# A vision tower on one core: up tiles of the feed-forward projected during the gate's search, most of them kept in DRAM

## The chip, the core and the metric

The kernel runs on one core of a Trainium2 chip. A core has a matrix engine (PE, TensorE), a vector engine (DVE), a scalar engine (ACT), GpSimd (POOL), and a queue engine (SP) that here only issues DMAs. Operands lie in SBUF, results of PE in eight banks of PSUM. The metric is the device time of one execution in microseconds. Three runs of the kernel before took 1360.43 to 1363.68 us, 1361.9 us in the median.

## What is computed

The reference is a small vision tower over 64 images of 96 x 96 pixels: a patch tokenizer (36 tokens of 192 features an image), attention with 12 heads of 16 (phase B below), two attention layers with 12 heads of 64 (phases C and D), and a gated feed-forward. Only this last layer is touched. Cut to what matters (x is the normalized input, 64 x 36 tokens):

```python
pooled = x.mean(1)                                  # 64 x 192, one row an image
ck     = relu(pooled @ w1.T) @ w2.T                 # 64 x 3072 gate values
probs  = softmax(ck, -1)
mask   = zeros_like(probs).at[b, top_k(probs, 768)].set(1.0)
hidden = relu(x @ w_mfc.T) * mask[:, None, :]       # 64 x 36 x 3072
out    = x_residual + hidden @ w_proj.T
```

## The kernel before, in words

The kernel keeps the tokens of all images in SBUF as h (22 groups of 108 tokens, three images each). Phases B, C and D are the attention layers, each closed by `phase_end`, a barrier of all five engines. During phase D the normalized input of the feed-forward is written transposed, as a rounded high part `f_xh` and a low part `f_xl`, since PE multiplies in a rounded format and the kernel wants more digits.

Phase E is the selection. PE and ACT compute the gate values into banks 0 to 2, half of the 3072 values of an image on each of two partitions, DVE takes the maximum, ACT the exponent, DVE scales them (`f_p`, 128 x 1536, line 1744). Then the 768th largest is searched bit by bit, 30 steps in `vector_select` (lines 1747 to 1764): DVE counts the values that reach the candidate (line 1750, `f_eq`), PE adds the two halves' counts in one small matmul (line 1665, into bank 7), DVE decides the bit with three small operations and so forms the next candidate. After the steps come two counts, a scan for ties, and two operations that make the mask `f_scan`; PE transposes it in 12 blocks (line 1674) into banks 0 to 2, and ACT copies it into `f_maskT` (line 1701). Beside this, SP loads the up weights (3 MB with one half doubled; `load_weights`) and then, when POOL is through with them, the down weights (2.3 MB). ACT rounds both to the high part and POOL subtracts to get the low part (`f_wu`, `f_wd`). The barrier of phase E follows.

The feed-forward walks six units of 4, 4, 4, 4, 3 and 3 groups (432 columns of tokens, at the end 324 and 252), and in each 24 tiles t of 128 hidden features. A tile m has an up half (five matmuls, `up` in `tensor_mlp`, lines 1814 to 1818, banks m mod 4), then on DVE relu and mask in one operation (`f_hid`, line 1891), on ACT the high part (line 1921), on POOL the low part (line 1935), and on PE a down half (five matmuls, lines 1829 to 1834) that adds into banks 4 and 5. The order on PE is up of tile m, down of tile m - 3 (`LAG`). There are four buffers each of `f_hid`, its high and low part: DVE waits for the parts of tile m - 4, ACT and POOL for its down half. After a unit, ACT and DVE copy banks 4 and 5 to `f_oT` (`take`), PE transposes them back (`back`, line 1845, into banks 6 and 7), DVE adds to h (`finish`), and SP stores the groups (`store`). In what order an engine works is the order of the code; the waits are counts on semaphores.

```python
        for m in range(len(order) + self.LAG):
            if m < len(order):
                up(m)
            if m >= self.LAG:
                u, g0, n, t = order[m - self.LAG]
                down(m - self.LAG)
```

## Time and profile before

| | us |
|---|---|
| median of three runs | 1361.9 |
| the profiled execution | 1363.47 |
| its span, first to last instruction | 1361.2 |
| PE busy in the span | 1183.3 (87%) |
| DVE busy | 956.3 (70%) |
| ACT busy | 880.7 (65%) |
| POOL busy | 436.9 (32%) |
| moved by DMA | 30.27 MB |

A busy time is the sum over an engine's instructions; a share of the whole span mixes stages that differ. The page also cuts the span into 40 slices of 34 us, with busy tenths for each engine and the granted clock of PE in tenths of full speed. The chain of waits follows back from the last instruction to what released each step. The profiled execution took 1363.47 us, 2.3 us more than its span.

### The profile page before, as it was taken

The numbers are of one execution on the slowest core, as the hardware profiler recorded it, in microseconds if no ns is written. First come the engines' busy times: TensorE is split into PE (matmuls) and PEld (weight loads), VectorE is DVE, ScalarE is ACT, GpSimd is POOL, SyncE is SP. The second block draws the span as 40 slices with busy tenths as digits, with TensorE's granted clock in tenths as the row PEclk, the third lists the DMA queues.
The fourth block names the chain that finished last, engine by engine and source line by source line (L and its number), as shares of the span: only waits on it lengthen the run. The fifth ranks groups of instructions, "written<-read, shape, count | busy, mean of one in ns | idle before, by whom it ended". The sixth has DMA issues, their size and how long they took to land.

```text
span 1361.2 us, 25095 instructions
## 1 busy us (share of the span) xinstructions
PE 1183.3 (87%) x8302; PEld 1043.3 (77%) x8302; DVE 956.3 (70%) x2350; ACT 880.7 (65%) x3172; POOL 436.9 (32%) x467
## 2 busy tenths in 40 slices
PE   6988879868999999998699999999830089999998
PEld 4986657647888888897589989899710079999998
DVE  4669988865888898896478888888758833333333
ACT  1757788854999999987498998998731022222232
POOL 0000130204323333320343443443224035555555
PEclk8999999896999999999899999999965589999999
DMA  9202011000000000000000000000031000000000
GB/s 371 109 1 72 1 47 25 1 1 0 2 1 2 1 1 2 1 2 1 12 1 1 1 1 2 1 1 1 1 93 70 0 1 1 11 10 11 1 11 13
DMA packets 7849, 30.27 MB, mean 22 GB/s; under 512 B 2094, under 2 KB 4894, under 8 KB 6174
## 3 DMA queue, kind: packets, MB, share of 16 engines
q1 hardware_dynamic: 7724, 28.69, 6.2%
q8 instruction: 68, 1.11, 0.3%
q14 instruction: 57, 0.47, 0.1%
HBM read 26.92 MB, written 1.77 MB: 21 GB/s over the span
## 4 chain that ended last, share of the span: by engine, by line
PE 61%; DVE 9%; ACT 6%; issue 1%; POOL 1%; POOLq 0%; ACTq 0%; DVEq 0%
PE bank L1466 6%; PE bank L1431 6%; DVE f_eq L1750 4%; PE bank L1395 4%; PE bank L1457 4%; PE bank L1440 3%; PE bank L1415 3%; PE bank L1399 3%; PE bank L1396 3%; PE bank L1397 3%; PE bank L1398 3%; ACT t_p L1211 2%; PE bank L1814 2%; PE bank L1829 2%; PE bank L1816 2%; PE bank L1815 2%
## 5 line engine op out<-in xcount | busy, mean ns | idle before, releaser
L1211 ACT ACTIVATE t_p<-bank,t_nmax 108x108 f32<-108x108 f32 x792 | 267.2, 354 | 40.2 <-DVE t_nmax L740 39.4
L1935 POOL TENSOR_TENSOR f_hid_lo<-f_hid,f_hid_hi 128x432 fp32r<-128x432 f32 (+2 forms) x144 | 145.8, 1013 | 160.6 <-ACT f_hid_hi L1921 160.6
L1891 DVE SCALAR_TENSOR_TENSOR f_hid<-bank,f_maskT 128x432 f32<-128x432 f32 (+2 forms) x144 | 80.3, 558 | 165.6 <-PE bank L1818 164.4
L1047 POOL TENSOR_TENSOR t_sq<-t_raw 108x768 f32<-108x768 f32 x88 | 140.9, 1602 | 168.7 <-ACT t_raw L1151 167.7
L1921 ACT CAST f_hid_hi<-f_hid 128x432 fp32r<-128x432 f32 (+2 forms) x144 | 73.9, 513 | 181.1 <-DVE f_hid L1891 181.1
L1431 PE MATMUL bank<-t_kS,t_qT 128*108 128x216 f32 (+1 forms) x660 | 179.1, 386 | 3.3 <-DVE h L331 2.5
L1211 ACT ACTIVATION_READ_ACCUMULATOR t_p<-bank,t_nmax 108x1 f32 x792 | 166.1, 210 | 0.0
L758 DVE TENSOR_TENSOR t_p<-t_p,t_rinv 108x432 f32<-108x432 f32 x198 | 160.4, 810 | 6.8
L740 DVE TENSOR_REDUCE t_nmax<-bank 108x4 f32<-108x432 f32 x198 | 119.5, 603 | 59.2 <-PE bank L1431 58.8
L1440 PEld LDWEIGHTS bank<-ident,t_p 108*108 108x108 f32 x792 | 86.7, 132 | 54.7 <-ACT t_pT L1219 35.1
L1440 PE MATMUL bank<-ident,t_p 108*108 108x108 f32 x792 | 107.4, 258 | 22.2 <-ACT t_pT L1219 21.0
L1431 PEld LDWEIGHTS bank<-t_kS,t_qT 128*108 128x108 f32 x660 | 110.6, 175 | 8.9 <-DVE h L331 2.5
L1219 ACT COPY t_pT<-bank 108x432 f32<-108x432 f32 x198 | 104.1, 527 | 11.4 <-PE bank L1440 10.4
L736 DVE TENSOR_TENSOR t_raw<-t_raw,t_rn 108x768 f32<-108x768 f32 x88 | 85.0, 966 | 16.4 <-ACT t_rn L1178 10.2
L1151 ACT COPY t_raw<-bank 108x384 f32<-108x384 f32 x176 | 86.3, 493 | 15.0 <-PE bank L1399 14.9
L1457 PE MATMUL bank<-t_pT,t_v 108*64 108x108 f32 (+1 forms) x1584 | 84.9, 263 | 6.6 <-issue 6.5
L1055 POOL TENSOR_TENSOR t_xl<-t_xt,t_xh 128x108 fp32r<-128x108 f32 x44 | 18.6, 422 | 213.9 <-DVE t_xh L711 213.9
L1457 PEld LDWEIGHTS bank<-t_pT,t_v 108*64 108x64 f32 (+1 forms) x1584 | 61.8, 127 | 33.2 <-issue 29.6
L1415 PE MATMUL bank<-ident,t_raw 108*128 108x108 f32 x528 | 78.7, 258 | 7.8 <-ACT t_kS L1193 3.3
L1415 PEld LDWEIGHTS bank<-ident,t_raw 108*128 108x128 f32 x528 | 66.1, 143 | 15.8 <-ACT t_kS L1193 3.9
L1665 PE MATMUL bank<-f_count,f_both 128*128 128x1 f16 x30 | 5.6, 186 | 70.5 <-DVE f_eq L1750 70.5
L391 PE MATMUL bank<-A_w,A_x 128*108 128x193 f32 x352 | 64.6, 339 | 1.9 <-DVE A_w L311 1.9
(227 smaller groups left out, 3250.6 us busy)
## 6 DMA issues: line engine op xcount, KB each, us to landing
A_x<-in_x SPq DMA_DIRECT2D x5, 1728.0 KB, 18.6
A_w<-in_tok_w SPq DMA_DIRECT2D x5, 768.0 KB, 7.2
f_raw_down<-in_w_proj SPq DMA_DIRECT2D x1, 2304.0 KB, 8.4
out_tokens<-h SPq DMA_DIRECT2D x21, 81.0 KB
f_raw<-in_w_mfc SPq DMA_DIRECT2D x1, 1536.0 KB, 7.3
f_raw<-in_w_mfc SPq DMA_DIRECT2D x2, 768.0 KB, 12.2
W_raw<-in_wC SPq DMA_DIRECT2D x1, 1159.0 KB
W_raw<-in_wC SPq DMA_DIRECT2D x2, 579.5 KB
```

The costliest lines, as they stand in the source:

```text
L736: dve.tensor_tensor(v, v, r, ALU.mult).then_inc(s["qn"], 1)
L740: dve.tensor_reduce(b.nmax[:, 4 * c:4 * c + 4], self.sbank[(3 * g + c) % 2][0:GT, 0:4 * GT].rearrange("p (a n) -> p a n", n=GT), AX.X, ALU ...
L758: dve.tensor_tensor(p, p, b.rinv[:, sl].unsqueeze(2).to_broadcast([GT, 4, GT]), ALU.mult).then_inc(s["pn"], 1)
L1047: pool.tensor_tensor(sq, v, v, ALU.mult).then_inc(s["sq"], 1)
L1151: act.copy(b.raw[k][:, 384 * c:384 * c + 384], src[0:GT, 0:384]).then_inc(s["Qev"], 1)
L1211: act.activation(b.p[g % 2][:, m, :], self.sbank[(3 * g + c) % 2][0:GT, n * GT:(n + 1) * GT], ACT.Exp, bias=b.nmax[:, m:m + 1], accum_out= ...
L1219: act.copy(b.pT[:, 4 * c:4 * c + 4, :], src.rearrange("p (a n) -> p a n", a=4)).then_inc(s["Tev"], 1)
L1415: mm = pe.transpose(o, b.raw[k][:, 128 * (3 * u + n):128 * (3 * u + n + 1)], I[0:GT, 0:GT])
L1431: mm = pe.matmul(o[0:GT, n * GT:(n + per) * GT], b.qT[g % 2][:, hd // per, :], b.kS[g % 2][:, hd:hd + per, :], start=masked, stop=True, sk ...
L1440: mm = pe.transpose(t[0:GT, n * GT:(n + 1) * GT], b.p[g % 2][:, 4 * c + n, :], I[0:GT, 0:GT])
L1457: mm = pe.matmul(self.pv[n][lo:hi, t * GT:(t + 1) * GT], b.v[g % 4][:, self.vd * hd:self.vd * (hd + 1)], b.pT[:, hd, :], start=True, stop= ...
L1935: pool.tensor_tensor(self.hid_lo[m % 4][:, c], self.hid[m % 4][:, c], self.hid_hi[m % 4][:, c].bitcast(F32), ALU.subtract).then_inc(s["lo" ...
```

## The change

Of the tiles of units 0 to 3, those with t not a multiple of 3 (64 of 96) have their up half computed in the selection: two after the sum of the exponents, two behind each of the 30 totals, two behind the sums for the ties (`early`, banks 3 to 5 in turn). ACT applies relu and writes each to one of eight slots in SBUF; SP stores 56 of them to DRAM (`spill`), and the last eight, the first kept ones of unit 0, stay in the slots. In the feed-forward SP reads the 56 back into the slots as they come free (`bring_back`), and for such a tile DVE multiplies the slot by the mask, which it reads from banks 0 to 2 of PSUM, in the order of the tiles. Up halves of the other tiles (`live`) use banks 6 and 3 in turn, later 0, 1, 6 and 3. The first two live up halves are computed in the selection too.

The up weights come in thirds of 1024 columns; two thirds are loaded by `load`, at the start of phase D, the last by `load_weights` at the start of the selection, and the down weights right after it without the wait for POOL. ACT rounds two thirds before the exponents and one after; the down weights are rounded and subtracted in four parts, between the evictions. The barrier of phase E is gone. The turning back of a unit is split into two lots of two groups (t = 1 and 6), in bank 7 (the last one in bank 0). The wait of PE for two casts at the start of phase C is dropped, and several semaphores are joined; the tokenizer's `s_wide` becomes a second count of `s_rows`.

```diff
-    phases = ("B", "C", "D", "E")
+    phases = ("B", "C", "D")
...
+        third = HID // 3
+        raw_of = lambda p, n: [p(f"f_raw{n}{m}", [128, third]) for m in two]
+        over = Plan_at(late, late.at)
+        self.w2 = over("f_w2", [12, HID])
+        self.raw = [raw_of(small, 0), raw_of(over, 1)]
...
+        unit = self.UNIT * GT
+        slot = lambda p, n: p(f"f_slot{n}", [128, unit])
+        self.slots = [slot(small, n) for n in range(5)]
...
+        self.raw_down = plan("f_raw_down", [128, HT, DIM])
+        self.raw.append(raw_of(plan, 2))
...
+        self.slots.append(slot(plan, 5))
+        below = Plan_at(small, first_raw_at)
+        self.slots += [slot(below, n) for n in range(6, self.SLOTS)]
...
+        self.order = list(self.tiles())
+        self.spilled = [m for m, (u, g0, n, t) in enumerate(self.order) if u < self.EARLY_UNITS and t % 3]
+        first = [m for m in self.spilled if self.order[m][0] == 0]
+        self.early = [m for m in self.spilled if self.order[m][0]] + first[self.SLOTS:] + first[:self.SLOTS]
+        self.stores = len(self.early) - self.SLOTS
+        self.stayed = nc.dram_tensor("spilled", (self.stores, 128, unit), F32, kind="Internal").ap()
+        self.moved = [sem(f"F_moved{n}") for n in range(self.SLOTS)]
...
+        self.load_third(sp, ins, 0, "rawU")
+        self.load_third(sp, ins, 1, "rawU")
+    def load_third(self, sp, ins, n, name):
+        cols = slice(n * HID // 3, (n + 1) * HID // 3)
+        a, b = self.raw[n]
+        sp.dma_start(a[:, :], ins["w_mfc"][0:128, cols]).then_inc(self.loaded[name], 16)
+        sp.dma_start(b[0:LO, :], ins["w_mfc"][128:192, cols]).then_inc(self.loaded[name], 16)
+        sp.dma_start(b[LO:128, :], ins["w_mfc"][128:192, cols]).then_inc(self.loaded[name], 16)
...
-        sp.dma_start(self.raw[0][:, :], ins["w_mfc"][0:128, :]).then_inc(self.loaded["rawU"], 16)
-        sp.dma_start(self.raw[1][0:LO, :], ins["w_mfc"][128:192, :]).then_inc(self.loaded["rawU"], 16)
-        sp.dma_start(self.raw[1][LO:128, :], ins["w_mfc"][128:192, :]).then_inc(self.loaded["rawU"], 16)
-        sp.wait_ge(self.s["wlo"], 2)
+        self.load_third(sp, ins, 2, "lastU")
         sp.dma_start(self.raw_down[:, :, :], ins["w_proj"]).then_inc(self.loaded["wdn"], 16)
...
+    def spill(self, sp):
+        for j in range(self.stores):
+            u, g0, n, t = self.order[self.early[j]]
+            w = self.columns(g0, n)
+            sp.wait_ge(self.s["relu"], j + 1)
+            sp.dma_start(self.stayed[j, :, 0:w], self.slots[self.slot(j)][:, 0:w])\
+              .then_inc(self.moved[self.slot(j)], 16)
+        for n in range(self.SLOTS):
+            sp.wait_ge(self.moved[n], 16 * self.stored(n))
+    def bring_back(self, sp, unit):
+        for q in range(self.SLOTS, len(self.spilled)):
+            m = self.spilled[q]
+            u, g0, n, t = self.order[m]
+            if u == unit:
+                w, k = self.columns(g0, n), self.slot(self.stores + q)
+                sp.wait_ge(self.s["hid"], self.spilled[q - self.SLOTS] + 1)
+                sp.dma_start(self.slots[k][:, 0:w], self.stayed[self.early.index(m), :, 0:w])\
+                  .then_inc(self.moved[k], 16)
...
+        def early(j):
+            u, g0, n, t = self.order[self.early[j]]
+            pe.wait_ge(s["low"], 2 * (t // self.THIRD + 1))
+            if j >= 3:
+                pe.wait_ge(s["relu"], j - 2)
+            self.project_up(pe, self.bank[3 + (j + 2) % 3], g0, n, t).then_inc(s["early"], 1)
+        pe.wait_ge(s["pre"], 2)
+        across(1, sm[:, 14:15], start=True, stop=True).then_inc(s["across"], 1)
+        early(0)
+        early(1)
         pe.wait_ge(s["padding"], 2)
         for n in range(self.BITS):
             pe.wait_ge(s["count"], n + 1)
             pe.matmul(self.bank[7][:, 0:1], self.both[:, :], self.count[:, 0:1], start=True, stop=True)\
               .then_inc(s["total"], 1)
+            early(2 * n + 2)
+            early(2 * n + 3)
         pe.wait_ge(s["eq"], 2)
         across(1, sm[:, 17:18], start=True, stop=False)
-        across(2, sm[:, 18:19], start=False, stop=True).then_inc(s["need"], 1)
-        pe.wait_ge(s["mask"], 1)
+        across(2, sm[:, 18:19], start=False, stop=True).then_inc(s["across"], 1)
+        for j in range(2 * self.BITS + 2, len(self.early)):
+            early(j)
+        pe.wait_ge(s["relu"], len(self.early) - 2)
+        self.up(pe, 0)
+        self.up(pe, 1)
+        pe.wait_ge(s["eq"], 6)
...
+        def high(n):
+            act.wait_ge(*((self.loaded["rawU"], 96) if n < 2 else (self.loaded["lastU"], 48)))
+            cols = slice(n * HID // 3, (n + 1) * HID // 3)
+            for m in range(2):
+                act.copy(self.wu[2 * m][:, cols], self.raw[n][m][:, :]).then_inc(s["high"], 1)
+        act.wait_ge(s["layers"], 1)
         act.activation(self.c1[:, 0:IMAGES], self.bank[6][0:12, 0:IMAGES], ACT.Relu, scale=1.0 / TOKENS)\
            .then_inc(s["c1s"], 1)
-        act.wait_ge(s["nmax"], 1)
+        high(0)
+        high(1)
+        act.wait_ge(s["pre"], 1)
         for c in range(self.half // 512):
             act.activation(self.p[:, 512 * c:512 * c + 512], self.bank[c][:, :], ACT.Exp, bias=sm[:, 7:8],
                            accum_out=sm[:, 8 + c:9 + c]).then_inc(s["exp"], 1)
-        act.wait_ge(self.loaded["rawU"], 48)
-        act.copy(self.wu[0][:, :], self.raw[0][:, :]).then_inc(s["whi"], 1)
-        act.copy(self.wu[2][:, :], self.raw[1][:, :]).then_inc(s["whi"], 1)
-        act.wait_ge(s["ck"], self.half // 512)
-        act.wait_ge(self.loaded["wdn"], 16)
-        act.copy(self.wd[:, :, 0:DIM], self.raw_down[:, :, :]).then_inc(s["dhi"], 1)
+        high(2)
+        for j, m in enumerate(self.early):
+            u, g0, n, t = self.order[m]
+            w, k = self.columns(g0, n), self.slot(j)
+            act.wait_ge(s["early"], j + 1)
+            if j >= self.SLOTS:
+                act.wait_ge(self.moved[k], 16 * len(range(k, j, self.SLOTS)))
+            elif j >= 6:
+                act.wait_ge(s["low"], 2)
+            act.activation(self.slots[k][:, 0:w], self.bank[3 + (j + 2) % 3][:, 0:w], ACT.Relu).then_inc(s["relu"], 1)
+            if j in (8, 12, 16, 20):
+                act.wait_ge(s["layers"], 1 + self.half // 512)
+                act.wait_ge(s["low"], 4)
+                act.wait_ge(self.loaded["wdn"], 16)
+                part = self.part(j // 4 - 2)
+                act.copy(self.wd[:, part, 0:DIM], self.raw_down[:, part, :]).then_inc(s["high"], 1)
...
+        for n in range(3):
+            cols = slice(n * HID // 3, (n + 1) * HID // 3)
+            for m in range(2):
+                pool.wait_ge(s["high"], 2 * n + m + 1)
+                pool.tensor_tensor(self.wu[2 * m + 1][:, cols], self.raw[n][m][:, :],
+                                   self.wu[2 * m][:, cols].bitcast(F32), ALU.subtract).then_inc(s["low"], 1)
...
+    def live(self, i):
+        turns = [m for m in range(len(self.order)) if m not in self.spilled]
+        of = []
+        for n, m in enumerate(turns):
+            masks = n < self.EARLY_UNITS * HT - len(self.spilled) + 6
+            of.append((6, 3)[n % 2] if masks else (0, 1, 6, 3)[n % 4])
+        past = [turns[n] for n in range(i) if of[n] == of[i]]
+        if not past and of[i] < 3:
+            past = [self.spilled[-1]]
+        return turns[i], self.bank[of[i]], past[-1] if past else None
+    def up(self, pe, i):
+        m, bank, past = self.live(i)
+        u, g0, n, t = self.order[m]
+        if past is not None:
+            pe.wait_ge(self.s["hid"], past + 1)
+        self.project_up(pe, bank, g0, n, t).then_inc(self.s["up"], 1)
...
+        turns = [m for m in range(len(order)) if m not in self.spilled]
         for m in range(len(order) + self.LAG):
-            if m < len(order):
-                up(m)
+            if m in turns[2:]:
+                self.up(pe, turns.index(m))
             if m >= self.LAG:
                 u, g0, n, t = order[m - self.LAG]
                 down(m - self.LAG)
-                if t == 1 and u:
-                    back(u - 1, self.UNITS[u - 1])
-        back(len(self.UNITS) - 1, self.UNITS[-1])
+                if u and t in (1, 6):
+                    back(u - 1, self.halves_of(u - 1)[t > 1])
+        for js in self.halves_of(len(self.UNITS) - 1):
+            back(len(self.UNITS) - 1, js)
...
+            if m in self.spilled:
+                k = self.spilled.index(m)
+                self.arrived(dve, k)
+                dve.wait_ge(s["mTev"], 2 * q + 2)
+                dve.tensor_tensor(split(self.hid[m % 4]), split(self.slots[self.slot(self.stores + k)]),
+                                  spread(self.bank[q][:, at:at + ni]), ALU.mult).then_inc(s["hid"], 1)
+            else:
+                i, bank, past = self.live(lives)
+                lives += 1
+                dve.wait_ge(s["up"], lives)
+                dve.wait_ge(s["mTev"], 2 * q + a + 1)
+                dve.scalar_tensor_tensor(out=split(self.hid[m % 4]), in0=split(bank), scalar=0.0,
+                                         in1=spread(self.maskT[:, t, i0:i0 + ni]), op0=ALU.max, op1=ALU.mult)\
+                   .then_inc(s["hid"], 1)
...
+        self.bring_back(sp, 0)
+        self.bring_back(sp, 1)
+        for u, n in enumerate(self.UNITS):
+            self.bring_back(sp, u + 2)
+            g0 = sum(self.UNITS[:u])
+            for g in range(g0, g0 + n):
+                rows = min(GT, total - g * GT)
+                sp.wait_ge(self.s["h"], 2 * (g + 1))
+                sp.dma_start(flat[g * GT:g * GT + rows, :], self.h[0:rows, g, :]).then_inc(stored, 16)
...
```

## Rows read from the trace of the kernel before

**Rows 1.** The page, 40 slices of the span: PE busy tenths, granted clock.

```profile
PE   6988879868999999998699999999830089999998
...
PEclk8999999896999999999899999999965589999999
```

**Rows 2.** Busy us by stretch: length, PE, PEld, DVE, ACT, POOL, PEclk, DMA share, GB/s.

```profile
160.00:170.00 10.00, 7.32 (x68) 5.69 (x69) 9.15 (x17) 7.38 (x36) 0.00 (x0) 1.00 0.01 2
1040.00:1060.00 20.00, 1.50 (x8) 0.84 (x8) 17.70 (x41) 0.00 (x0) 9.61 (x2) 0.50 0.00 0
1151.10:1199.04 47.94, 47.94 (x250) 45.82 (x249) 17.06 (x33) 13.70 (x25) 26.83 (x25) 1.00 0.03 8
1158.00:1159.00 1.00, 1.00 (x7) 0.96 (x6) 0.96 (x4) 0.00 (x0) 0.34 (x1) 1.00 0.56 161
```

**Rows 3.** Timeline (start us, us, engine, line, operation, out<-in), a search step.

```profile
1078.04 0.19 PE L1665 MATMUL bank<-f_count,f_both 128*128 128x1 f16 x1 [2.31 <-DVE f_eq L1750]
...
1078.66 1.81 DVE L1750 TENSOR_SCALAR_CACHE_REDUCE f_eq<-f_p,f_word 128x1536 bf16<-128x1536 f32 x1
...
1081.16 1.81 DVE L1750 TENSOR_SCALAR_CACHE_REDUCE f_eq<-f_p,f_word 128x1536 bf16<-128x1536 f32 x1
```

**Rows 4.** Timeline, one tile of unit 0 in the feed-forward.

```profile
1124.48 0.36 PE L1814 MATMUL bank<-f_xh,f_wu 128*128 128x432 f32 x1
...
1124.97 1.11 POOL L1935 TENSOR_TENSOR f_hid_lo<-f_hid,f_hid_hi 128x432 fp32r<-128x432 f32 x1 [0.85 <-ACT f_hid_hi L1921]
...
1125.66 0.61 DVE L1891 SCALAR_TENSOR_TENSOR f_hid<-bank,f_maskT 128x432 f32<-128x432 f32 x1 [1.36 <-PE bank L1818]
...
1126.44 0.36 PE L1814 MATMUL bank<-f_xh,f_wu 128*128 128x432 f32 x1
```

**Rows 5.** The chain of waits (start us, us, what), turning back a unit.

```profile
1154.06 0.87 PE bank L1845 x8
```

**Rows 6.** Timeline, the first matmuls of the feed-forward.

```profile
1097.40 0.65 ACT L1701 COPY f_maskT<-bank 128x256 f32<-128x256 f32 x2 [0.21 <-PE bank L1674]
...
1098.67 0.56 PE L1815 MATMUL bank<-f_xh,f_wu 128*128 128x432 f32 x1
...
1101.91 0.37 PE L1814 MATMUL bank<-f_xh,f_wu 128*128 128x432 f32 x1
...
1103.89 0.36 PE L1829 MATMUL bank<-f_hid_hi,f_wd 128*128 128x432 f32 x1
```

**Rows 7.** Groups by line and shape, feed-forward: busy us, mean ns | idle before.

```profile
L1935 POOL TENSOR_TENSOR f_hid_lo<-f_hid,f_hid_hi 128x432 fp32r<-128x432 f32 x96 | 107.2, 1118 | 132.7 <-ACT f_hid_hi L1921 132.7
...
L1891 DVE SCALAR_TENSOR_TENSOR f_hid<-bank,f_maskT 128x432 f32<-128x432 f32 x96 | 58.3, 607 | 126.0 <-PE bank L1818 126.0
...
L1921 ACT CAST f_hid_hi<-f_hid 128x432 fp32r<-128x432 f32 x96 | 53.1, 553 | 135.9 <-DVE f_hid L1891 135.9
```

**Rows 8.** Timeline, PE near the end of phase D.

```profile
971.43 3.45 PE L1466 MATMUL bank<-oD,t_oT 128*108 128x192 f32 x12 [1.28 <-ACT t_oT L1226]
```

**Rows 9.** The page's DMA issues: out<-in, count, KB each, us to landing.

```profile
f_raw_down<-in_w_proj SPq DMA_DIRECT2D x1, 2304.0 KB, 8.4
```

**Rows 10.** Timeline, a stretch of phase B, then the first part of the selection.

```profile
151.91 5.10 POOL L489 TENSOR_TENSOR wC_lo<-W_raw,wC_hi 128x2318 fp32r<-128x2318 f32 x1 [48.25 <-ACT wC_hi L468]
...
154.46 3.01 DVE L758 TENSOR_TENSOR t_p<-t_p,t_rinv 108x432 f32<-108x432 f32 x1
...
1004.19 0.69 ACT L1685 ACTIVATE f_p<-bank,f_small 128x512 f32<-128x512 f32 x1 [7.37 <-DVE f_small L1738]
...
1007.37 1.02 DVE L1744 TENSOR_SCALAR f_p<-f_p,f_small 128x1536 f32<-128x1536 f32 x1
...
1010.51 2.75 ACT L1689 CAST f_wu<-f_raw 128x3072 fp32r<-128x3072 f32 x1 [4.20 <-DMA f_raw<-in_w_mfc]
...
1013.40 6.69 POOL L1706 TENSOR_TENSOR f_wu<-f_raw,f_wu 128x3072 fp32r<-128x3072 f32 x1 [17.60 <-ACT f_wu L1689]
...
1013.66 1.81 DVE L1750 TENSOR_SCALAR_CACHE_REDUCE f_eq<-f_p,f_word 128x1536 bf16<-128x1536 f32 x1
```

182 lines of the change are left out of this document (91 added, 91 removed).

## The prediction

> **What bounds the kernel now.** I read the slices of the page first [rows 1]. The slices in which PE falls to 3, 0 and 0 tenths are the selection; behind them come some 260 us of feed-forward with PE at 8 or 9. The busy times by stretch say the same [rows 2]: from 1040 to 1060 us DVE is busy for 17.7 of 20 us and PE for 1.5, at a granted clock of 0.50 (the lower level, 1.2 GHz); from 1151.10 to 1199.04 us, unit 1 of the feed-forward, PE is busy throughout at 1.00 (2.4 GHz), while POOL has 26.8 of 47.9 us. So there are two bounds side by side: a serial search on DVE, in which PE has nothing to do, and then PE alone. The timeline of one search step [rows 3]: a count of 1.81 us on DVE, 0.19 us PE, two small DVE operations, and the next count starts 2.50 us after the last. Thirty steps are 75 us of nearly free PE.
>
> A tile of the feed-forward [rows 4]: the first up matmuls of neighbouring tiles start at 1124.48 and 1126.44, 1.96 us apart, for ten matmuls at a pitch of 0.196 us. A group of five (one up or one down half) is 0.98 us. Check: unit 1 took 47.94 us [rows 2]; less 0.87 us of turning back [rows 5] it is 47.07 / 24 = 1.961 us for a tile. At the lower clock the pitch is 0.36 us: nine of them lie between 1098.67 and 1101.91 us [rows 6]; a group is 1.80 us.
>
> **The change, part by part.**
>
> (a) Up halves moved. 64 of the 96 up halves of units 0 to 3 go into the search. They are all 432 columns wide: 64 x 0.981 = 62.8 us less on PE behind the search. PE is the bound there, so it counts in full if no other engine becomes the bound. Three tiles (one live, two kept) now take PE 4 groups, 3.92 us. POOL needs 3 x 1.118 = 3.35 us, DVE 3 x 0.607, ACT 3 x 0.553 [rows 7]. POOL has 0.57 us left in 3.92. By the order of the code POOL may be up to four tiles ahead of the down half, and a live tile's chain (0.61 + 0.55 + 1.12 us and hops, some 2.5 us) must be over before PE has done its next four groups (3.9 us). It fits.
>
> (b) What they cost in the search. PE gets two tiles behind each total: 10 x 0.196 + 0.19 = 2.15 us in a step of 2.50 us, at the upper clock. That leaves 0.35 us. At the lower clock it would be 10 x 0.36 + 0.19 = 3.8 us: each step 1.3 us and more longer. Which level is granted decides the case. Less than 4 us of continuous work brought a matmul from 0.56 to 0.37 us at 1101.91 us [rows 6]. The clock stood at 1.00 in a stretch where PE was busy for 7.32 of 10 us [rows 2]; the search would be 86% busy with gaps of 0.35 us. After a gap of 1.28 us twelve matmuls took 3.45 us, the lower level [rows 8]. From about 1007 us PE works without a pause (tiles 0 and 1 at the lower clock, 3.6 us, end near 1010.7; the first total is due after the scaling at 1007.37, 1.02 us, and a count of 1.81, near 1010.4 [rows 10]), so I put 0.3 us on the start, with 1.5 us as the upper bound. The total matmul itself may be quicker at the upper clock: bounds 0 and half of its 0.19 us in each of 30 steps; I take 0.05 x 30 = 1.5 us gained. If tiles crowd the total by 0.25 us in each step, 7.5 us are lost: that is the other bound.
>
> (c) ACT and the stores. ACT gets two evictions a step, each like the 0.55 us conversion of 432 columns [rows 7], and in four steps a quarter of the down weights' copy (4608 columns; by the 2.75 us for 3072 [rows 10] some 1.0 us): at most 2.1 us of 2.50. The stores are 221 KB each; two a step are 177 GB/s. A burst of stores of the output ran at 161 GB/s at a DMA share of 0.56, so up to 287 GB/s when busy throughout [rows 2]. They fit, and eight slots give 10 us of slack. The returns are asked for eight kept tiles ahead (some 15 us), against 8.4 us for the landing of ten times the bytes [rows 9]. On SP the returns for unit u+2 stand ahead of the stores of unit u, which delays only output that nobody waits for: from unit 2 on there are none. Both transfers: nothing on the path.
>
> (d) Weights. Up weights in thirds: two of the loads (2 MB) move into phase D, on queues that are idle there; the six conversions on ACT (about 1 us each, a third of 2.75 [rows 10]) start near 996.9 us: four end by 1000.9, before ACT's first exponent at 1004.19. POOL's six subtractions (a third of 6.69 us, 2.25 us each) run from about 998 to 1012 us. Here is the only collision that I see. The row at 154.46 us [rows 10] shows a DVE multiply with both inputs in SBUF take 3.01 us in place of 0.61, up to 157.0, just as the POOL operation that began at 151.91 ended. The scaling of p at 1007.37 us (1.02 us for 1536 elements, twice the pace of the counts) is on the chain, and POOL's fourth subtraction ends near 1007.0, its fifth starts near 1007.3. Bounds: 0, or two whole POOL operations, 4.5 us. I take one, +2.3 us. The counts themselves took 1.81 us while POOL was in its 6.69 us operation as well as without it [rows 3, 10], so they cost nothing.
>
> The Trainium skill has the rule, in "SBUF — State Buffer", section "Who interferes with whom": a DVE instruction in a 2-port mode, or with two SBUF inputs, and a GpSimd one that reads SBUF exclude each other, whoever is first. The row agrees for two inputs. Applied to kept tiles: their multiply reads a slot in SBUF and the mask in PSUM, so by that rule POOL is left alone; with the mask in SBUF the sum would be 20 us worse (rival 2).
>
> (e) The start of the feed-forward. Before, four up halves were done at 1103.89 us and 284 groups were left. After, PE has two live up halves done and starts the downs when ACT, done with the masks at 1098.05 us [rows 6], has converted tile 0 (1098.6 us). At the lower clock, each down waiting for POOL: down 0 ends about 1100.5, down 1 at 1102.3, down 2 at 1103.3. Left: 288 - 64 - 2 - 3 = 219 groups. Gain against before, parts (a) and (e) together: (284 - 219) x 0.981 + (1103.89 - 1103.3) = 64.4 us. The tail of the selection on DVE stays as it is: four groups (tiles 62, 63, two live ones) run under it from 1088.4; even with the first at the lower clock they end before 1094.5. The mask transposes could then run at 1.4 in place of 2.8 us: 0 to -1.4, I take 0. The removed barrier is inside this part.
>
> (f) The rest: joined semaphores and the split turning back (same 8 transposes a unit, in two lots) cost nothing: each lot is followed by matmuls already released. In units 4 and 5 nothing changes but two banks for the first six tiles; there an up half waits for a multiply released three groups earlier.
>
> **Sum.** 1363.47 - 64.4 - 1.5 + 0.3 + 2.3 = 1300.2 us for the profiled execution. That one is 1.6 us above the median of its runs, 1361.9; on that scale the forecast is 1298.6, said as 1299. The unknown parts alone give 1293 to 1309 (lock -2.3/+2.2, crowded steps +9, transposes -1.4, faster totals -1.5, and some 1 us for the start).
>
> **Rivals.**
> 1. Steps crowded: PE's 2.15 us plus restart gaps exceed what is free before the next total. For: only 0.35 us of slack, and each tile waits for an eviction and a weight third. Against: the pitch of 0.196 held over whole units. +7.5 us and more, 1307 to 1312.
> 2. POOL becomes the bound of units 0 to 3. If kept tiles' multiplies (0.61) and POOL's operation exclude each other, three tiles take 3.35 + 1.2 = 4.6 us in place of 3.92: 32 x 0.65 = 21 us, 1320. Against: the live multiply (one input in PSUM) overlapped POOL at 1.12 us unstretched [rows 4, 7]. Store traffic at only 120 GB/s would cost about the same (12.4 MB in 103 us).
> 3. The change does not do what it says in time: the search stays at 1.2 GHz because PE stops at each total. A step is then about 3.9 us, 30 x 1.4 = 42 us given back: 1341.
> 4. Slower than before: the lower clock holds in the search and also in units 0 to 3, since PE waits there for POOL's results behind a short chain. A group costs 0.82 us more. After the 42 us of rival 3, 21 us are left, which 26 of the 219 groups use up: from there on the kernel is slower. With all 128 groups of units 0 to 3 it is +105 us, 1446. Against: 1.00 in every stretch of the feed-forward, and PE has work queued there.
>
> **How the numbers follow.** Forecast 0.74 (1293 to 1306), rival 1 0.10, rival 2 0.06, rival 3 0.06, rival 4 0.03, and 0.01 for a gain that vanishes by several of these. The range 1291 to 1313 takes the forecast with its bounds and rival 1. Faster by over 0.2% (what a measurement of this kernel can tell from no change) 0.96, within 0.01, slower 0.03.
>
> **What would show it.** Search steps still 2.45 to 2.50 us apart at a granted clock of 1.00; PE near 86% busy in them; the multiply of p stretched to about 3.3 us; units 1 to 3 at 24 + 8 groups, 31.4 + 0.9 = 32.3 us each, with PE full; POOL near 83% in them and still 1.12 us an operation; units 4 and 5 as before. Wrong it would be by steps of 2.7 us or more, a clock of 0.5 in the search, units over 34 us, or PE waiting for a returned slot.

## The result, and the profile after

The changed kernel took 1300.86 us in the median (1299.40 to 1303.14), the kernel before 1361.97: a ratio of 0.9553, 95% interval 0.9535 to 0.9570. The forecast was 1299, the range 1291 to 1313. The profiled execution took 1300.88 us, against 1300.2 of the sum.

The page after: span, the slices of PE and DVE, the granted clock and the share of the DMA engines, to be read beside [rows 1].

```profile
span 1299.1 us, 25559 instructions
...
PE   6998779895899999999869999999996898999998
...
DVE  5668989875788888889547888888874888444434
...
PEclk9999999897899999999989999999998899999999
DMA  9302002000000000000030000000003342334100
```

The two empty slices of PE are gone. DVE is as busy in the search as before, and the span ends 62 us sooner. The DMA engines, idle in the search before [rows 2], are at 2 to 4 tenths there and up to the end of unit 2 of the feed-forward.

Busy time by stretch (columns as in [rows 2]): the first two search steps, the other 28 steps, the tail of the selection, units 1 and 2 of the feed-forward.

```profile
1010.33:1016.74 6.41, 4.67 (x16) 3.86 (x16) 4.42 (x10) 1.48 (x3) 2.00 (x1) 0.54 0.26 97
1016.74:1086.40 69.66, 64.45 (x310) 52.36 (x309) 61.82 (x140) 33.61 (x61) 11.26 (x8) 1.00 0.46 169
1086.40:1097.28 10.88, 7.91 (x33) 6.82 (x32) 10.68 (x8) 2.12 (x4) 0.00 (x0) 0.84 0.01 2
...
1136.00:1168.14 32.14, 32.14 (x171) 30.75 (x169) 15.84 (x33) 13.42 (x25) 26.21 (x25) 1.00 0.38 112
1168.14:1200.30 32.16, 32.16 (x170) 30.77 (x169) 15.86 (x33) 13.46 (x25) 26.23 (x25) 1.00 0.42 121
```

The 28 steps take 69.66 us, 2.488 each, with PE at 93% and the upper clock; they carry 56 of the early tiles. Unit 1 takes 32.14 us in place of 47.94, PE full, POOL at 26.2 us, 82%. The forecast had 2.45 to 2.50 and 32.3. (From its turning back to the next, unit 3 took 33.73 us, 1200.30 to 1234.03: PE runs three tiles ahead, and in this stretch it does five up halves of unit 4, all live, where a unit of kept tiles has two.)

The groups of the feed-forward by line and shape, for [rows 7]: POOL's subtraction, DVE's multiply of a kept tile, DVE's relu and mask of a live one.

```profile
L2090 POOL TENSOR_TENSOR f_hid_lo<-f_hid,f_hid_hi 128x432 fp32r<-128x432 f32 x96 | 104.7, 1119 | 80.8 <-ACT f_hid_hi L2076 80.6
...
L2040 DVE TENSOR_TENSOR f_hid<-f_slot,bank 128x432 f32<-128x432 f32 x64 | 35.8, 595 | 1.3 <-ACT f_hid_hi L2076 0.8 <-POOL f_hid_lo L2090 0.5
L2047 DVE SCALAR_TENSOR_TENSOR f_hid<-bank,f_maskT 128x432 f32<-128x432 f32 x32 | 19.4, 608 | 59.3 <-PE bank L1922 52.5 <-POOL f_hid_lo L2090 5.6 <-ACT f_maskT L1806 1.3
```

POOL's operation is as long as before (1119 ns, 1118 before), kept multiplies beside it or not: with the mask in PSUM they do not meet.

The page's DMA issues, the stores and the returns, with the median us to landing.

```profile
spilled<-f_slot SPq DMA_DIRECT2D x56, 216.0 KB, 1.9
f_slot<-spilled SPq DMA_DIRECT2D x56, 216.0 KB, 2.5
```

The start of the search, on the timeline (start us, us, engine, line, operation; idle before it and who ended it in brackets), for [rows 3, 10].

```profile
1006.93 5.40 POOL L1814 TENSOR_TENSOR f_wu<-f_raw,f_wu 128x1024 fp32r<-128x1024 f32 x2 [0.15 <-ACT f_wu L1770]
1006.99 3.13 DVE L1850 TENSOR_SCALAR f_p<-f_p,f_small 128x1536 f32<-128x1536 f32 x1
...
1010.33 1.81 DVE L1856 TENSOR_SCALAR_CACHE_REDUCE f_eq<-f_p,f_word 128x1536 bf16<-128x1536 f32 x1
...
1012.30 0.16 PE L1743 MATMUL bank<-f_count,f_both 128*128 128x1 f16 x1 [1.74 <-DVE f_eq L1856]
...
1012.90 1.81 DVE L1856 TENSOR_SCALAR_CACHE_REDUCE f_eq<-f_p,f_word 128x1536 bf16<-128x1536 f32 x1
...
1015.71 0.56 PE L1922 MATMUL bank<-f_xh,f_wu 128*128 128x432 f32 x1
```

POOL began 0.06 us before DVE, and the scaling of p took 3.13 us in place of 1.02: the collision of part (d). PE had by then finished tiles 0 and 1 at the lower clock (0.56 us a matmul) and stood idle for 1.74 us until the delayed first total at 1012.30. The next two tiles ran at the lower clock again (the last of their matmuls at 1015.71), with the second total behind them, for which DVE waited 1.57 us: the second count begins at 1012.90 and the third at 1016.74, 3.84 us later.

Stage by stage, all from the timelines (us; the first row before, the second after, the last the difference):

| | first matmul of the selection to the scaling | scaling to first count | 30 steps | tail to the mask transposes | from there to the last addition | sum |
|---|---|---|---|---|---|---|
| before | 11.45 | 1.23 | 75.06 | 10.89 | 264.87 | 363.50 |
| after | 11.45 | 3.34 | 76.07 | 10.88 | 199.93 | 301.67 |
| difference | 0 | +2.11 | +1.01 | 0 | -64.94 | -61.83 |

The sum of a row, from the first matmul of the selection to the last addition to h, is called the stretch below. It leaves out what lies before the selection, which the edits hardly touch: the selection began between 993.7 and 997.9 us in the executions profiled, in no order that follows the edits. Still it is one execution of each kernel, and the granted clock differs from one to the next: what that does to single steps is told under e1_no_lock.

### The profile page after: what moved, and what is told of

Same layout as the page of the kernel before. It is cut to its first block, busy times and chain, and to the rows that moved or that the text cites. A ratio compares the mean times of both kernels' runs of the same rounds, so it can differ in the third digit from the quotient of the medians.

```text
span 1299.1 us, 25559 instructions
## 1 busy us (share of the span) xinstructions
PE 1191.0 (92%) x8302; PEld 1042.0 (80%) x8302; DVE 953.1 (73%) x2350; ACT 913.1 (70%) x3243; POOL 437.0 (34%) x477
## 3 DMA queue, kind: packets, MB, share of 16 engines
q1 hardware_dynamic: 24460, 53.47, 12.4%
## 4 chain that ended last, share of the span: by engine, by line
PE 59%; DVE 9%; ACT 7%; issue 2%; POOL 1%; POOLq 0%; DVEq 0%; ACTq 0%
PE bank L1463 7%; PE bank L1428 6%; PE bank L1392 4%; DVE f_eq L1856 4%; PE bank L1454 4%; PE bank L1437 3%; PE bank L1412 3%; PE bank L1396 3%; PE bank L1393 3%; PE bank L1395 3%; PE bank L1394 3%; ACT t_p L1208 2%; PE bank L1965 2%; PE bank L1961 2%; PE bank L1966 2%; PE bank L1962 2%
## 5 line engine op out<-in xcount | busy, mean ns | idle before, releaser
L2047 DVE SCALAR_TENSOR_TENSOR f_hid<-bank,f_maskT 128x432 f32<-128x432 f32 (+2 forms) x80 | 41.4, 518 | 100.3 <-PE bank L1922 92.9
L1792 ACT ACTIVATE f_slot<-bank 128x432 f32<-128x432 f32 x64 | 34.0, 531 | 49.0 <-PE bank L1922 49.0
```

## The experiments

All are edits on the changed kernel. The table has the median time, the ratio to the kernel before with its interval, and the stretch of the profiled execution with its difference to that of the changed kernel (301.67 us).

| run | us | ratio | stretch, us |
|---|---|---|---|
| changed kernel | 1300.86 | 0.9553 (0.9535 to 0.9570) | 301.67 |
| e3_all_live | 1361.67 | 0.9984 (0.9973 to 0.9994) | 362.90, +61.23 |
| e4_three_units | 1316.75 | 0.9660 (0.9646 to 0.9674) | 316.61, +14.94 |
| e1_no_lock | 1297.39 | 0.9513 (0.9501 to 0.9525) | 297.76, -3.91 |
| e2_mask_sbuf | 1302.86 | 0.9555 (0.9543 to 0.9567) | 302.76, +1.09 |
| e5_three_a_step | 1312.63 | 0.9627 (0.9614 to 0.9640) | 312.58, +10.91 |
| e10_one_a_step | 1332.93 | 0.9770 (0.9757 to 0.9783) | 333.11, +31.44 |
| e6_no_dram | 1302.24 | 0.9551 (0.9538 to 0.9564) | 301.29, -0.38 |
| e8_late_thirds | 1305.59 | 0.9571 (0.9556 to 0.9586) | 308.55, +6.88 |
| e11_barrier_back | 1301.85 | 0.9540 (0.9527 to 0.9553) | 302.16, +0.49 |
| e9_gap_filled | 1301.41 | 0.9546 (0.9533 to 0.9559) | 301.95, +0.28 |
| e7_more_kept | 1295.00 | 0.9496 (0.9483 to 0.9509) | 293.97, -7.70 |

**Is the gain the moved PE work, and all of it?** Two kernels keep the rest of the change and take early tiles away.

e3_all_live: no tile is kept.

```diff
-    EARLY_UNITS = 4
+    EARLY_UNITS = 0
...
+        act.wait_ge(s["low"], 4)
+        act.wait_ge(self.loaded["wdn"], 16)
+        for n in range(4):
+            act.copy(self.wd[:, self.part(n), 0:DIM], self.raw_down[:, self.part(n), :]).then_inc(s["high"], 1)
```

(The four down conversions stand alone, since there are no evictions to put them between.)

> Everything of the change but the early tiles: thirds of the weights, no barrier, two live up halves in the selection, split turning back; no tile is kept. The theory that the gain is PE work moved: 64 x 0.981 = 62.8 us come back, less 1.3 us of the stretched step and plus 1 to 2 us of a cold start of the feed-forward: 1363 to 1364, so the rest of the change is worth nothing or costs 1 to 2 us (2.1 of it the locked scaling). Rival (the barrier, the four-part weights and the start carry part of the gain): clearly under 1360.

e4_three_units:

```diff
-    EARLY_UNITS = 4
+    EARLY_UNITS = 3
...
-        pe.wait_ge(s["relu"], len(self.early) - 2)
+        pe.wait_ge(s["relu"], len(self.early) - 1)
```

> The changed kernel with early tiles for units 0 to 2 alone: 48 in place of 64, 40 stored. Theory (each early half is worth its 0.981 us of PE behind the search, wherever it stands): 16 x 0.981 = +15.7 us, 1316.6; steps stay 2.49 us, the last eight are empty. Rival (the gain saturates because POOL or the returns limit the units): clearly less than +15.7.

Without kept tiles the kernel is back within 0.2% of the kernel before, a little under the 1363 to 1364 us expected. Neither run has the stretched second step, so the tiles are counted by the last column but one of the stage table, from the mask transposes to the last addition (199.93 us in the changed kernel). It is 262.18 us in e3_all_live, 62.25 us more for 64 tiles, 0.973 each; the sum had 62.8. In e4_three_units it is 216.12 us, 16.2 more for 16 tiles, 1.01 each. By both, and by e10_one_a_step below, the gain is proportional to the groups that are moved, within the 1 us or so that the clock at the start of the feed-forward can shift, and nothing saturates. What is left of the -64.94 us, 2.69, came with the rest of the change (two live up halves in the selection, no barrier); its parts were not told apart. All the rest together, with the +2.1 us of the collision in it, is -0.60 us, 362.90 against 363.50.

**Does the collision cost what it seems to?** e1_no_lock lets POOL wait for the scaled p before its last two up subtractions.

```diff
         for n in range(3):
...
+            if n == 2:
+                pool.wait_ge(s["pre"], 4)
```

> One line more than the changed kernel: POOL holds back its two subtractions of the last third of the up weights until DVE has scaled p. In the changed kernel the scaling took 3.13 us in place of 1.02 while POOL worked from 1006.93 on, and the second search step began 3.84 us after its first, at the lower clock. Port theory: the scaling is back at 1.02 us (-2.1 us), PE then has no idle 1.7 us before the first total, so the next step is not stretched either (-1.3 us); together -3.4 us, about 1297.4 us. Rival A (the stretch of step 1 has nothing to do with the delay, PE is simply at the lower clock there): -2.1 us, 1298.8. Rival B (something else than POOL slows the scaling): 0, 1300.9.

The timeline of its first steps:

```profile
1007.78 1.02 DVE L1852 TENSOR_SCALAR f_p<-f_p,f_small 128x1536 f32<-128x1536 f32 x1
...
1008.88 4.70 POOL L1816 TENSOR_TENSOR f_wu<-f_raw,f_wu 128x1024 fp32r<-128x1024 f32 x2 [1.32 <-DVE f_p L1852]
...
1009.00 1.81 DVE L1858 TENSOR_SCALAR_CACHE_REDUCE f_eq<-f_p,f_word 128x1536 bf16<-128x1536 f32 x1
...
1011.82 1.81 DVE L1858 TENSOR_SCALAR_CACHE_REDUCE f_eq<-f_p,f_word 128x1536 bf16<-128x1536 f32 x1
...
1014.95 1.81 DVE L1858 TENSOR_SCALAR_CACHE_REDUCE f_eq<-f_p,f_word 128x1536 bf16<-128x1536 f32 x1
```

The scaling is at 1.02 us with POOL starting behind it, and the kernel is faster by 0.4%. That settles what slowed the scaling, 2.1 us. But the second half of the expectation failed: the first two steps are 2.82 and 3.13 us long, since PE still works at the lower clock there, so of the 1.3 us only 0.5 came back, and without any delay the cold start still costs 1.0 us. Nor is the delay what makes it dear. e4_three_units has the same code up to this point, the same scaling of 3.13 us and the same idle 1.74 us of PE before the first total. Its second and third count:

```profile
1012.18 1.81 DVE L1858 TENSOR_SCALAR_CACHE_REDUCE f_eq<-f_p,f_word 128x1536 bf16<-128x1536 f32 x1
...
1014.67 1.81 DVE L1858 TENSOR_SCALAR_CACHE_REDUCE f_eq<-f_p,f_word 128x1536 bf16<-128x1536 f32 x1
```

Its second step is 2.49 us long: the matmuls behind the first total already ran at the upper clock (granted 0.91 from 1009.62 to 1014.67). In the other executions with two tiles a step and the delayed scaling, the second step was 3.39 (e6_no_dram) to 3.85 us. So the stretch of this step is a matter of when the clock rises, and that differs from one execution to the next.

The rest of the 3.9 us came from the start of the feed-forward (1.4 us), where this execution had no fall of the clock. This cannot be put down to the edit: e2_mask_sbuf and e5_three_a_step, without it, had no fall there either. Three microseconds of that start, by stretch (columns as in [rows 2]), first in e1_no_lock:

```profile
1101.00:1104.00 3.00, 3.00 (x16) 2.72 (x15) 0.72 (x2) 0.56 (x1) 3.00 (x4) 1.00 0.60 147
```

Then in the changed kernel, at 0.68:

```profile
1103.00:1106.00 3.00, 3.00 (x12) 2.83 (x11) 0.11 (x1) 0.60 (x2) 3.00 (x4) 0.68 0.59 147
```

**Is the mask read from PSUM what keeps POOL free?** e2_mask_sbuf reads it from SBUF.

```diff
-                                  spread(self.bank[q][:, at:at + ni]), ALU.mult)
+                                  spread(self.maskT[:, t, i0:i0 + ni]), ALU.mult)
```

> The changed kernel, with the mask of the kept tiles read from its copy in SBUF in place of PSUM; same numbers computed. Port theory: this multiply now has two inputs in SBUF and excludes POOL's operation, so three tiles take POOL and DVE 3 x 1.119 + 2 x 0.595 = 4.55 us in place of 3.92 us of PE: 32 x 0.63 = 20 us more, 1321 us, and unit 1 some 37 us in place of 32.1. Rival (the source of the mask does not matter, as DVE has 50% idle): 0, 1301.

The two groups in its feed-forward, up to the end of unit 3:

```profile
L2090 POOL TENSOR_TENSOR f_hid_lo<-f_hid,f_hid_hi 128x432 fp32r<-128x432 f32 x95 | 124.8, 1350 | 61.8 <-ACT f_hid_hi L2076 61.8
...
L2040 DVE TENSOR_TENSOR f_hid<-f_slot,f_maskT 128x432 f32<-128x432 f32 x64 | 70.0, 1131 | 0.8 <-ACT f_hid_hi L2076 0.8
```

They do meet: POOL's mean goes from 1119 to 1350 ns and DVE's from 595 to 1131. But this costs the kernel 1.1 us of the stretch and nothing that the timed ratio tells, not 20 us. (The 1.1 us are too few: this execution had no fall of the clock at the start of the feed-forward. From the third live up half to the last addition it took 193.90 us, the changed kernel 191.79: 2.1 us are the price, and the timed ratio cannot tell so little.) I had counted POOL's operation and DVE's two as one after the other, 4.55 us for three tiles. From one turning back to the next (1137.26, 1169.95, 1202.65) a unit takes 32.70 us in place of 32.16, 4.09 us for three tiles in place of 4.02 (turning back included), and three of POOL's operations are 4.05 us: they lose 0.23 us each, while the loss of DVE, which has time to spare, is larger. So POOL, busy for 31.6 of the 32.7 us, is just at the bound, and the 20 us of the prediction were far off. With the mask in PSUM each of the two has its own length, as the rows of the changed kernel above show.

**How much does a step hold?** e5_three_a_step puts three tiles behind each of the first 20 totals.

```diff
-            early(2 * n + 2)
-            early(2 * n + 3)
+            for j in range(3 * n + 2, min(3 * n + 5, 62)):
+                early(j)
```

> The changed kernel with the same 64 early tiles, but three behind each of the first 20 totals and none behind the last ten. Theory (a step is as long as the longer of DVE's 2.49 us and PE's groups plus its total): 3 x 0.981 + 0.18 = 3.12 us in the first 20, so +0.63 x 20 = +12.7 us, about 1313.5; this is what crowded steps cost. Rival (PE's work hides further, for it may run behind the next count): 0, 1301.

One of its steps:

```profile
1031.06 0.18 PE L1745 MATMUL bank<-f_count,f_both 128*128 128x1 f16 x1
...
1031.29 0.17 DVE L1865 SCALAR_TENSOR_TENSOR bank<-bank,f_bits 128x1 uint32<-128x1 f32 x1 [0.79 <-PE bank L1745]
...
1031.68 1.81 DVE L1858 TENSOR_SCALAR_CACHE_REDUCE f_eq<-f_p,f_word 128x1536 bf16<-128x1536 f32 x1
...
1034.74 1.81 DVE L1858 TENSOR_SCALAR_CACHE_REDUCE f_eq<-f_p,f_word 128x1536 bf16<-128x1536 f32 x1
```

The total starts at 1031.06, right behind the third tile's matmuls, and DVE waits 0.79 us for it: a step of 3.06 us (1031.68 to 1034.74), just three groups of 0.98 and 0.12 us. Two groups and the total leave some 0.4 us of a step of 2.49. The 30 steps take 88.16 us in place of 76.07, 12.1 us more, near the 12.7 expected (the stretch shows 10.9, as the start of the feed-forward had no fall of the clock here); the empty last ten steps give nothing back. This is rival 1 at work: it begins somewhere between two and three tiles a step.

e10_one_a_step asks for the other side.

```diff
-    EARLY_UNITS = 4
+    EARLY_UNITS = 2
...
-            early(2 * n + 2)
-            early(2 * n + 3)
+            early(n + 2)
...
-        pe.wait_ge(s["relu"], len(self.early) - 2)
+        pe.wait_ge(s["relu"], len(self.early))
```

> Early tiles for units 0 and 1 alone (32), one behind each total, so that PE has 0.98 + 0.18 us in a step of 2.49 us. It asks what clock is granted with half the work. If the clock is held by long enough pauses alone (1.3 us here), the steps are at the lower level: a tile then takes 1.80 us and still fits, the steps stay 2.50 us, and the time is 1300.9 + 32 x 0.981 = 1332.3 us less the 1.3 us of the stretched step. If the upper clock holds, the same time: only the granted clock tells the two apart. A third outcome, that totals wait for a slow tile, would give more than 1334.

Two stretches of its search:

```profile
1020.00:1040.00 20.00, 15.45 (x48) 10.93 (x48) 17.75 (x41) 5.20 (x9) 2.78 (x2) 0.66 0.24 89
...
1060.00:1080.00 20.00, 13.39 (x49) 9.37 (x48) 17.76 (x41) 5.82 (x10) 2.79 (x2) 0.82 0.13 45
```

The granted clock is 0.66 and 0.82 in the mean, so both levels occur within the search, while steps stay at 2.49 us. The time is that of 32 tiles less: from the mask transposes to the last addition it is 232.50 us, 32.6 more, 1.02 each. (Of this some part is the clock, which was lower here at the start of the feed-forward; the 31.44 us of the stretch are less because no step is stretched.) One tile a step is not hurt by the lower clock (five matmuls of 0.36 us fit), but two are only free at the upper one, which PE, at 93%, kept for all 28 steps of the changed kernel. Rival 3 needed a fall of the clock there, and the short stop at each total did not bring it.

**Are the transfers free?** e6_no_dram issues neither stores nor returns. ACT and DVE no longer wait for slots to be stored or filled. The kept tiles of the feed-forward then multiply whatever a slot holds, so their part of the result is left out of the computation.

```diff
-            sp.wait_ge(self.s["relu"], j + 1)
-            sp.dma_start(self.stayed[j, :, 0:w], self.slots[self.slot(j)][:, 0:w])\
-              .then_inc(self.moved[self.slot(j)], 16)
...
-                sp.wait_ge(self.s["hid"], self.spilled[q - self.SLOTS] + 1)
-                sp.dma_start(self.slots[k][:, 0:w], self.stayed[self.early.index(m), :, 0:w])\
-                  .then_inc(self.moved[k], 16)
...
-            eng.wait_ge(self.moved[k], 16 * (self.stored(k) + q // self.SLOTS))
+            eng.wait_ge(self.s["relu"], len(self.early))
```

> The changed kernel without the 56 stores and the 56 returns: the slots are overwritten and the feed-forward multiplies what stands in them, so this part of the computation is wrong in its values and the same in its instructions. Theory (24.8 MB of transfers lie wholly beside the work): within 0.5 us of 1300.9. Rival (they cost something by late returns, or by slowing the engines' SBUF accesses): 2 us or more faster.

From 1136 to 1230 us (units 1 to 3), first e6_no_dram, then the changed kernel:

```profile
1136.00:1230.00 94.00, 94.00 (x495) 90.14 (x494) 45.02 (x95) 37.79 (x71) 76.32 (x71) 1.00 0.04 12
```

```profile
1136.00:1230.00 94.00, 94.00 (x497) 90.07 (x495) 44.66 (x94) 38.08 (x71) 76.39 (x71) 1.00 0.35 101
```

The DMA share is the column that moves; the busy times of the engines are the same within 1%, and so is the ratio. The 0.38 us of the stretch lie in the second search step (3.39 us in place of 3.84), which varies with the clock; from the mask transposes on it took 199.99 us against 199.93.

**Does the sooner load matter?** e8_late_thirds loads all three thirds at the start of the selection.

```diff
-        self.load_third(sp, ins, 0, "rawU")
-        self.load_third(sp, ins, 1, "rawU")
...
+        self.load_third(sp, ins, 0, "rawU")
+        self.load_third(sp, ins, 1, "rawU")
         self.load_third(sp, ins, 2, "lastU")
```

> The changed kernel with all three thirds of the up weights loaded at the start of the selection, none in phase D. Theory (the sooner loads are on the path: ACT converts two thirds before the exponents, in the order of its code): they land some 7 us after the selection begins, the conversions (3.9 us) end near 1007 in place of 1000.2, the exponents start 3 to 4 us later than 1003.81, and the collision of the scaling with POOL stays: 1304 to 1305. Rival (the loads were early for nothing, as other work covers them): 1301.

```profile
1006.08 3.88 ACT L1770 CAST f_wu<-f_raw 128x1024 fp32r<-128x1024 f32 x4 [11.42 <-DMA f_raw<-in_w_mfc]
...
1009.87 0.68 ACT L1779 ACTIVATE f_p<-bank,f_small 128x512 f32<-128x512 f32 x1
...
1013.05 2.04 DVE L1850 TENSOR_SCALAR f_p<-f_p,f_small 128x1536 f32<-128x1536 f32 x1
```

Yes. ACT gets its first third at 1006.08, 12.4 us after the first matmul of the selection (993.65), and the exponents wait behind its four conversions, until 1009.87; the scaling of p comes at 1013.05, 19.4 us after that matmul in place of 11.45. The stretch is 6.9 us longer, more than expected, because I had put the landing at 7 us. The median is 1305.6, 4.7 us more; the ratios say 2.5 us, with intervals that overlap. Against e11_barrier_back, timed beside the same runs of the kernel before, the intervals do not overlap (0.9556 to 0.9586, and 0.9527 to 0.9553), though that kernel has an extra barrier. So the thirds at the start of phase D are the better ones; the size lies between 2.5 and 7 us.

**The barrier.** e11_barrier_back has `phase_end` of all five engines again.

```diff
-    phases = ("B", "C", "D")
+    phases = ("B", "C", "D", "E")
...
         F.tensor_select(pe)
+        phase_end(pe, "E")
         F.tensor_mlp(pe)
```

> The changed kernel with the barrier of all five engines behind the selection put back, SP's part behind its last store. Theory (the barrier is short, and only the first multiply, which now starts after the first of six mask copies, is held back until the last): the first down half comes 1.0 to 1.5 us later, 1302.2. Rival (nothing, since ACT's copies hold everything back anyway): 1300.9. Rival (SP's last store, at the end of a chain of DMAs, is waited for by all): 1303 or more.

```profile
1099.34 1.53 PE L1765 MATMUL bank<-ident,f_scan 128*128 128x128 f32 x12 [0.95 <-DVE f_scan L1892]
...
1103.25 0.58 PE L1966 MATMUL bank<-f_hid_hi,f_wd 128*128 128x432 f32 x1 [2.38 <-ACT f_hid_hi L2081]
```

The first down half comes 3.91 us after the first transpose, in the changed kernel 2.94 (1097.28 to 1100.22): the barrier does hold it back by 1.0 us. To the last addition 0.5 us are left of it, and the timed ratios overlap. What the barrier costs, 0 to 1 us, this measurement cannot tell from nothing.

**What lowers the clock in the tail?** Here the trace of the changed kernel did not fit my picture. Its PE in the tail of the selection and at the start of the feed-forward:

```profile
1090.13 0.61 PE L1725 MATMUL bank<-f_small,f_halves 128*128 128x1 f32 x4 [2.02 <-DVE f_eq L1876]
...
1090.88 0.36 PE L1919 MATMUL bank<-f_xh,f_wu 128*128 128x432 f32 x1
...
1091.07 0.37 PE L1920 MATMUL bank<-f_xl,f_wu 128*128 128x432 f32 x1
...
1091.95 0.56 PE L1918 MATMUL bank<-f_xh,f_wu 128*128 128x432 f32 x1
...
1092.31 0.56 PE L1919 MATMUL bank<-f_xh,f_wu 128*128 128x432 f32 x1
...
1094.79 0.36 PE L1921 MATMUL bank<-f_xh,f_wu 128*128 128x432 f32 x1
...
1097.28 1.53 PE L1760 MATMUL bank<-ident,f_scan 128*128 128x128 f32 x12 [0.95 <-DVE f_scan L1887]
...
1100.22 0.46 PE L1961 MATMUL bank<-f_hid_hi,f_wd 128*128 128x432 f32 x1 [1.41 <-ACT f_hid_hi L2076]
```

After an idle time of 2.02 us (from 1088.11 to 1090.13) the next matmuls are still at the upper clock, 0.19 us apart at 1090.88 and 1091.07. Then, in the midst of continuous work, the pitch goes to 0.36 us (1091.95, 1092.31), and back near 1094.8. In e1_no_lock the same gap was followed by the lower clock at once:

```profile
1088.33 0.81 PE L1725 MATMUL bank<-f_small,f_halves 128*128 128x1 f32 x4 [2.04 <-DVE f_eq L1878]
...
1089.50 0.56 PE L1921 MATMUL bank<-f_xh,f_wu 128*128 128x432 f32 x1
```

e9_gap_filled moves two tiles into the idle time.

```diff
+        early(2 * self.BITS + 2)
+        early(2 * self.BITS + 3)
         pe.wait_ge(s["eq"], 2)
...
-        for j in range(2 * self.BITS + 2, len(self.early)):
+        for j in range(2 * self.BITS + 4, len(self.early)):
```

> The changed kernel, with tiles 62 and 63 put ahead of the sums for the ties in place of behind them, so that PE has no idle 2.0 us there. In the changed kernel PE ran at the lower clock from about 1091.3 to 1094.6 us, in the midst of matmuls, after that gap, and again from 1101.5 to 1104.8 at the start of the feed-forward. Clock theory: no fall in the tail (granted 1.00), which costs or gains nothing as DVE is the bound there; if the second fall also hangs on it, the feed-forward is 1.3 us shorter: 1299.6. Rival (the falls have other causes): the tail at 0.84 mean as before, 1300.9.

Its first 6.4 us of the tail, the time behind them, and a stretch of the start of the feed-forward:

```profile
1086.29:1092.70 6.41, 6.33 (x33) 5.41 (x31) 6.34 (x5) 2.13 (x4) 0.00 (x0) 1.00 0.01 3
1092.70:1097.18 4.48, 0.03 (x2) 0.01 (x1) 4.35 (x4) 0.00 (x0) 0.00 (x0) 1.00 0.00 0
1098.00:1104.00 6.00, 4.82 (x16) 3.90 (x15) 3.36 (x6) 4.17 (x11) 3.42 (x4) 0.50 0.34 92
```

The fall in the tail is gone, in this one execution. But the gap is only moved: PE is now idle for nearly all of the 4.48 us behind it, and in the six microseconds at the start of the feed-forward the clock is at the lower level, where it costs. Nothing is gained, and what makes the clock fall where it does stays open.

**A better version.** e7_more_kept puts the three things together: POOL waits for the scaling, tiles 62 and 63 go into the gap, and four more tiles are kept, computed where PE was idle behind the sums.

```diff
-        self.spilled = [m for m, (u, g0, n, t) in enumerate(self.order) if u < self.EARLY_UNITS and t % 3]
+        self.spilled = [m for m, (u, g0, n, t) in enumerate(self.order) if u < self.EARLY_UNITS and (t % 3 or (u and t == 12) or (u == 3 and t == 18))]
...
-        pe.wait_ge(s["relu"], len(self.early) - 2)
         self.up(pe, 0)
+        pe.wait_ge(s["relu"], len(self.early))
```

> Three edits on the changed kernel: POOL's last two up subtractions wait for the scaling of p; tiles 62 and 63 go ahead of the sums for the ties, into the 2.0 us in which PE waits; and four more tiles are kept (68), computed in the tail of the selection, where PE still has idle time under DVE's scan. Theory: -3.5 us of the first (as measured), -4 x 0.981 = -3.9 us of PE work, and the clock does not fall in the tail: about 1293.5, 1292.5 if the start of the feed-forward is at the upper clock. Rival (six groups behind the sums end after the mask is ready and delay it, or five kept tiles in a row make PE wait for POOL): 1297 or more.

The tail of its selection, and unit 2:

```profile
1084.98:1095.90 10.92, 10.34 (x53) 9.21 (x52) 10.72 (x9) 4.26 (x8) 0.00 (x0) 1.00 0.09 34
1164.50:1195.72 31.22, 31.22 (x165) 29.87 (x164) 15.77 (x33) 13.48 (x25) 26.21 (x25) 1.00 0.45 132
```

PE is busy for 10.34 of the 10.92 us of the tail, at the upper clock throughout, and a unit with 17 kept tiles is one group shorter (31.22 us). 1295.0 us is 0.6% less than the changed kernel, with intervals that do not touch; the stretch is 7.7 us shorter, the timed median 5.9. Most of this is POOL's wait. Against e1_no_lock, which has that alone, the stretch is 3.8 us shorter, as 4 x 0.98 would have it, but the timed intervals of the two overlap (0.9501 to 0.9525, and 0.9483 to 0.9509).

## Why the prediction was right

- **(a) and (e), moved halves and start: -64.4 foreseen, -64.94 measured.** e3_all_live and e4_three_units confirm the price of a half. Counted from the first mask transpose (the selection ended 2.7 us later than in the kernel before), I had down 0 ending after 5.95 us and down 2 after 8.75. Down 0 ended after 4.9, since the transposes ran at the upper clock (1.53 us in place of 2.82), which I had put at 0, and down 2 after 8.14, with the clock at the lower level from about 1101.5 to 1104.8. The 0.6 us that the start was better than the sum are about the whole difference between -64.4 and -64.94.
- **(b) the search: -1.2 foreseen, +1.0 measured.** Both terms were mis-sized. The total is only 0.012 us a step sooner at the upper clock, 0.35 us in all and not 1.5. And the cold start cost 1.3 us and not 0.3: I had counted tiles 0 and 1 at the lower clock, but tiles 2 and 3 ran at it too, with the second total behind them. The delay of (d) is not the reason, since without it the cost was 1.0 us (e1_no_lock), and with it none in e4_three_units. The bound of 1.5 held it.
- **(c) stores and returns: 0 foreseen, 0 measured** (e6_no_dram). They landed in 1.9 and 2.5 us. Of PE's share in the steps, 93% and not 86%, a part is only how a row counts: the last matmul before a pause has 0.35 us and not its pitch of 0.20. Ten pitches and 0.12 us for the total are 2.08 of 2.49 us, 84%.
- **(d) weights: +2.3 foreseen, +2.11 measured,** by the mechanism named; e1_no_lock shows that it is POOL. POOL's operation had begun only 0.06 us before the scaling, so an equally good account of the change could have had none of this loss; I took one operation, near the middle of the bounds, and that it came out is in part luck. In e8_late_thirds, where the scaling began in the midst of a row of POOL's operations, it took 2.04 us, so 1.0 us was lost and not a whole operation. The row that I took for a model [rows 10] I also misread: the multiply of 154.46 us ended at 157.47, 0.46 us behind POOL's operation and not with it.
- The rule of the Trainium skill cited there ("SBUF — State Buffer", section "Who interferes with whom") has POOL and DVE exclude each other. The scaling fits it: its 2.11 us of delay is about the length of one POOL operation (2.25 us). For a multiply with two inputs in SBUF e2_mask_sbuf does not: POOL's operations lost 0.23 us each, where full exclusion would have set three tiles at 4.55 us and 4.09 was measured. What is measured is a slowing of both, and my 20 us for rival 2 rested on the exclusion.
- **(f)** Unit 4 took 35.78 us from turning back to turning back, 35.67 before (1296.46 to 1332.13): 0.1 us, so nothing to speak of, as said.
- **Rivals 3 and 4** needed a lower clock under two tiles a step. It stayed at 1.00 from the third step on, but in e10_one_a_step, with half of that work, it did not.

That the sum came so near, 1300.2 for the profiled execution against 1300.88, is in part luck. Within the stretch the forecast was 1.5 us too low (2.2 us by (b), less 0.5 by the start and 0.2 by (d)), and what lies before the selection and behind the last addition, where nothing was forecast, was 0.8 us shorter than in the execution before. The distance of the medians, 1299 and 1300.9, is mostly the 1.6 us that were taken off because the profiled execution before was that far above its median; the one after was not.

## What to carry to other kernels

Work of a bound engine can be moved into a serial search of another one for its full price per piece, as long as the pieces fit a step. Whether they do can be computed beforehand from pitch and step: two tiles (2.08 of 2.49 us) cost nothing, three (3.06 us) lengthened each step by about as much as they did not fit. Where in between the edge lies was not tried. The round trip through DRAM was free because it ran on DMA engines that were nearly idle there (a share of 0.04 without it, 0.35 with it). Look at what the moved helpers (conversions, subtractions) now run beside: the largest loss here, 2.1 us, came from an operation on POOL that began 0.06 us ahead of one on the chain, and one wait removed it.
